# A selective scan with a routed feed-forward: u and the softplus sums transposed apart, and their product made in place out of PSUM

## The chip, the cores and the metric

One core of a Trainium2 chip runs the whole block. The metric is device time in microseconds. A core has five engines that run their own instruction streams in order and meet at semaphores: TensorE (PE, matrix products and transposes, results in PSUM), VectorE (DVE), ScalarE (ACT, activations), GpSimd (POOL) and SyncE (SP, which issues DMAs here).

## The reference, cut to what matters

```python
def step(state, inp):                      # over time, for each of 4 batches
    d, b, c, u = inp                       # d = softplus(dt), u = silu(conv(x))
    dA = jnp.exp(d[..., None] * A)         # 512 channels x 16 states
    state = state * dA + (d * u)[..., None] * b[:, None, :]
    y = jnp.einsum('bdn,bn->bd', state, c)
    return (state, y)
...
y = (moveaxis(ys) + D[None, :, None] * x) * silu(z)
x = x + tanh(g_xattn[0]) * y               # then x + tanh(g_ffn[0]) * (16 experts, 2 of them per token, + shared)
```

`d` comes from a rank 16 projection: `dt = softplus(dt_proj_w @ dt_low + dt_proj_b)`. All of it is fp32, 4 batches of 512 time steps.

## The kernel before, in words

The first half of the kernel is the scan. Channels stand on the 128 partitions in four groups j, time along the free dimension (512). A batch has 64 items i = 4n + j, for state n (16) and group j (4), and each engine has its part of an item:

- ScalarE makes `dA` of the item from `dts` (L1162, `decay`), and after the decay of j = 2 the inputs of the whole state n: `dbuT = duT * B`, four operations with time on the partitions (L1173, `input_terms`). That is why d*u is needed transposed, as `duT`.
- TensorE transposes `dbuT` back to channels, into one of two PSUM banks `dbu_ps` (L767, `step`), then adds the product of the item five before (LAG = 5) to `y_ps` by a transpose (L785, `add_y`), then does what `pieces` has for the item.
- VectorE scans, `hst = scan(dA, dbu_ps)` (L1476), then its `pieces`.
- GpSimd multiplies by C, `prod = hst * cbc` (L573, `products`). `prod` has four slots, so the product of item i waits until TensorE has added that of item i-4. `dA` and `hst` have eight, so ScalarE can be eight items ahead of VectorE.

While batch b is scanned, the `pieces` of items 8 to 63 prepare batch b+1 in two PSUM banks of their own, `mp[0]` and `mp[1]`: convolution and projection (items 8 to 34), silu (ScalarE, item 40), the projection to dt, B and C (`x_proj`, 37 to 40), and then for each group j the softplus and d*u. Each bank is used in a fixed order: a use begins when the one before is read (`bank_free`, `misc_full`, `misc_read`; `HEAD`, `LOOP`, `ut_use`, `bt_use`, `dut_use` number the uses). For group j, with the items at which each engine has its part in the kernel before:

- `dt_proj` (TensorE, L742, items 42, 46, 50, 54) into `mp[0]`.
- `softplus_parts` (ScalarE, L1135 to L1141, items 46, 50, 54, 58): abs, relu, exp, log. It waits for the sum dt of two groups before.
- `round_part` (VectorE, L1452, items 44, 48, 52, 56) makes `sp_t`, and `log_part` (GpSimd, L554 and L557, after the product of the same items) corrects the logarithm by it.
- `dt_part` (VectorE, L1458, items 48, 52, 56, 60): `dts = sp_r + sp_l`.
- `du_part` (VectorE, L1469, items 49, 53, 57, 61): `du = dts * xs`, where `xs` is u.
- `du_transposes` (TensorE, L749, items 50, 54, 58, 62) into `mp[1]`, and `du_to_time` (ScalarE, L1145, items 57, 61 and items 0 and 1 of the next batch) copies them to `duT`.

`b_transposes` (TensorE, item 42) and `b_to_sbuf` (VectorE, item 43) bring B to `BT` through `mp[1]`. `skip_part` (GpSimd, after the batch) multiplies `xs` by D in place. At items 2 to 5 of the next batch VectorE finishes the batch before (`post`, L1485). Batches 0 to 2 are one loop on each engine (`Fori`), batch 3 is written out after it and has no preparation. The second half of the kernel, the experts, comes after all of this.

Of the kernel before, what the change touches and what calls it, by code (L numbers as in the profile page):

```python
# [18 lines left out]
def flamingo_block(nc, x, ctx_in, g_xattn, g_ffn, in_proj_w, conv_w, conv_b, x_proj_w, dt_proj_w,  # L19
# [33 lines left out]
    with ExitStack() as top:  # L53
# [31 lines left out]
        xs = s1("xs", [P, ND, L])  # L85
        sp_t = s1("sp_t", [P, L])
        sp_u = s1("sp_u", [P, 2, L])
# [238 lines left out]
        HEAD0, HEAD1 = 8, 8  # L326
        LOOP0, LOOP1 = 7, 13

# [12 lines left out]
        def dt_use(bp):  # L341

            return bp * LOOP0 + HEAD0 - 4

        def bt_use(bp):
# [187 lines left out]
        def _(pool):  # L533
# [16 lines left out]
            def log_part(bp, j):  # L550

                q = bp * ND + j
                pool.wait_ge(sp_round, q + 1)
                pool.tensor_tensor(sp_t[:], sp_t[:], sp_u[:, j % 2, :], ALU.subtract).then_inc(sp_err, 1)  # L554
                pool.wait_ge(sp_ln, q + 1)
                pool.wait_ge(sp_err, q + 1)
                pool.tensor_tensor(sp_l[:, j % 2, :], sp_l[:, j % 2, :], sp_t[:],  # L557
                                   ALU.subtract).then_inc(sp_log, 1)

            def skip_part(bp):  # L560
                pool.wait_ge(du_ready, (bp + 1) * ND)
                pool.sem_inc(wait_carrier, 1)
                for j in range(ND):
                    pool.tensor_scalar(xs[:, j, :], xs[:, j, :], Dv[:, j:j + 1], 1.0, ALU.mult,
                                       ALU.mult).then_inc(skip_ready, 1)

            def products(b, n, bp=None):
                pool.wait_ge(c_loaded[n % 2], 16 * (b * (NS // 2) + n // 2 + 1))
                for j in range(ND):
                    i = b * ITEMS + n * ND + j  # L570
                    pool.wait_ge(scanned, i + 1 + RING)
                    pool.wait_ge(prod_used, i + 1)
                    pool.tensor_tensor(prod[:, prod_slot(n, j), :], hst[:, slot_of(n, j), :], cbc[:, n % 2, :],  # L573
                                       ALU.mult).then_inc(prod_ready, 1)
                    if bp is not None and 11 <= n < 15 and j == 0:
                        log_part(bp, n - 11)

# [101 lines left out]
        def _(pe):  # L679
# [64 lines left out]

            def du_transposes(use, bp, j):
                pe.wait_ge(du_ready, bp * ND + j + 1)
                bank_free(1, use)
                for t in range(NL):
                    last = tr(mp[1][:, t * P:(t + 1) * P], du[:, j % 2, t * P:(t + 1) * P], ident[:])  # L749
                last.then_inc(misc_full[1], 1)  # L750
# [38 lines left out]
            def pieces(b, n, j):  # L789
# [19 lines left out]
                if 37 <= i < 41:  # L809
                    x_proj(xp_use(bp), bp, i - 37, i - 36)  # L810
                if 10 <= n < 14 and j == 2:
                    dt_proj(dt_use(bp) + n - 10, n - 10)
                if i == 42:
                    b_transposes(bt_use(bp), bp)
                if 12 <= n < 16 and j == 2:
                    du_transposes(dut_use(bp) + n - 12, bp, n - 12)

# [54 lines left out]
            first_steps(0)  # L872
            with pe.Fori(0, NB - 1) as b:
                for n in range(2, NS):
# [198 lines left out]
        def _(act):  # L1073
# [68 lines left out]

            def du_to_time(bp, j):
                act.wait_ge(misc_full[1], dut_use(bp) + j + 1)
                nc.scalar.copy(par(duT, bp)[:, :, j * P:(j + 1) * P],  # L1145
# [42 lines left out]
            def pieces(bp, n, j):  # L1188
# [5 lines left out]
                if i == 40:  # L1194
                    silus(bp, (misc_read[0], base0(b) + 3))
                if 11 <= n < 15 and j == 2:
                    softplus_parts(bp, n - 11)
                if 14 <= n < 16 and j == 1:
                    du_to_time(bp, n - 14)
                if n == 0 and j < 2:  # L1200
                    du_to_time(bp, j + 2)

# [35 lines left out]
            with act.Fori(0, NB - 1) as b:  # L1238
                for n in range(2, NS):
                    step(b, n, b + 1)  # L1240
                step(b + 1, 0, b + 1)
                step(b + 1, 1)
# [124 lines left out]
        def _(dve):  # L1367
# [78 lines left out]
            def round_part(bp, j):  # L1446

                q = bp * ND + j
                if not (isinstance(q, int) and q < 1):
                    dve.wait_ge(sp_log, q)  # L1450
                dve.wait_ge(sp_exp, q + 1)
                V.tensor_scalar(sp_t[:], sp_u[:, j % 2, :], 1.0, -1.0, ALU.add, ALU.add).then_inc(sp_round, 1)  # L1452

# [6 lines left out]

            def du_part(bp, j):

                q = bp * ND + j
                dve.wait_ge(dt_ready, q + 1)
                dve.wait_ge(silu_done, bp + 1)
                if j >= 2:
                    dve.wait_ge(misc_full[1], dut_use(bp) + j - 1)
                dve.sem_inc(wait_carrier, 1)
                V.tensor_tensor(du[:, j % 2, :], par(dts, bp)[:, j, :], xs[:, j, :], ALU.mult).then_inc(du_ready, 1)  # L1469

# [24 lines left out]
            def pieces(b, n, j):  # L1495
# [16 lines left out]
                if i == 41:  # L1512
                    x_proj_to_sbuf(bp)
                if i == 43:
                    b_to_sbuf(bp)
                if 11 <= n < 15 and j == 0:
                    round_part(bp, n - 11)
                if 12 <= n < 16 and j == 0:
                    dt_part(bp, n - 12)
                if 12 <= n < 16 and j == 1:  # L1520
                    du_part(bp, n - 12)

# [398 lines left out]
```

## Time and profile before

| | us |
|---|---|
| median of 3 runs | 1107.25 (1105.29 to 1111.7) |
| the profiled execution | 1106.53 |
| its span | 1104.9 |
| first scan / last scan of the first half begins | 60.0 / 512.3 |
| busy: PE / DVE / ACT / POOL | 920.2 / 728.1 / 611.2 / 594.0 |

The span is what the profile covers. Busy time is summed over the whole span, and the two halves of the kernel have different limits: the scan half ends at about 521 us. In timelines a row starts with its start and its duration, neighbouring operations of one kind are merged (x4), and what stands in brackets is the idle time before and what ended it.

### The profile page before, as it was taken

What the parts mean: (1) busy time and instruction counts of PE and PEld (TensorE: products, weight loads), DVE (VectorE), ACT (ScalarE), POOL (GpSimd) and SP (SyncE); (2) the same over time, 40 slices, a digit from 0 to 9 for tenths busy, and PEclk for the clock granted to TensorE, in tenths of its full rate; (3) what the DMA queues carried; (4) which work ended last, traced back from release to release, by engine and by line L of the source; (5) the groups of instructions that cost most, each with busy time, mean ns of one, the idle gap of its engine ahead of it and who ended that gap; (6) DMA issues with size and microseconds to landing.
All of it is one profiled execution on the core that took longest, in us unless ns stands there. A gap on an engine that the chain in (4) does not pass through costs nothing.

```text
span 1104.9 us, 22746 instructions
## 1 busy us (share of the span) xinstructions
PE 920.2 (83%) x5388; PEld 776.6 (70%) x5389; DVE 728.1 (66%) x1023; ACT 611.2 (55%) x1037; POOL 594.0 (54%) x521
## 2 busy tenths in 40 slices
PE   6589876998689877974799989699999999973787
PEld 3267655765567566753799979698988898862775
DVE  4769798878888788998544467354544545444467
ACT  4697997599778977993322222243444544432211
POOL 4557796878967796996100007334344424420254
PEclk9579998999999978998899999899999999995789
DMA  8105111331105113110311118645556656653376
GB/s 254 40 20 191 59 36 33 138 109 30 39 28 199 49 29 109 56 48 20 117 38 38 51 36 296 242 137 204 184 197 216 216 203 233 206 176 111 116 220 236
DMA packets 67432, 137.08 MB, mean 124 GB/s; under 512 B 9392, under 2 KB 15024, under 8 KB 67248
## 3 DMA queue, kind: packets, MB, share of 16 engines
q1 hardware_dynamic: 54736, 105.66, 28.5%
q0 software_dynamic: 8960, 29.37, 7.4%
q10 hardware_dynamic: 3680, 1.39, 0.6%
q8 instruction: 24, 0.39, 0.1%
q14 instruction: 32, 0.26, 0.1%
HBM read 163.53 MB, written 42.07 MB: 186 GB/s over the span
## 4 chain that ended last, share of the span: by engine, by line
PE 40%; issue 4%; DVE 4%; POOL 3%; DMA 1%; ACT 1%; DVEq 0%; POOLq 0%
PE psY L956 12%; PE psG L920 11%; PE psU L920 10%; PE psT L913 3%; POOL slot_in L625 3%; PE psHT L934 3%; DVE x_tok L1864 1%; ACT xh L1290 1%; DMA gbuf<-slot_out,posi 0%; PE dbu_ps L767 0%; DVE hl L1676 0%; DVEq L1841 0%; DVE xl L1682 0%; PE y_ps L785 0%; POOL gbuf L672 0%
## 5 line engine op out<-in xcount | busy, mean ns | idle before, releaser
L573 POOL TENSOR_TENSOR prod<-hst,cbc 128x512 f32<-128x512 f32 x256 | 333.0, 1327 | 84.8 <-PE y_ps L785 66.9
L1476 DVE TENSOR_TENSOR_SCAN hst<-dA,dbu_ps 128x512 f32<-128x512 f32 x256 | 304.0, 1208 | 67.8 <-PE dbu_ps L767 57.8
L767 PE MATMUL dbu_ps<-ident,dbuT 128*128 128x128 f32 x1024 | 169.9, 292 | 38.5 <-ACT dbuT L1173 16.8
L767 PEld LDWEIGHTS dbu_ps<-ident,dbuT 128*128 128x128 f32 x1024 | 124.9, 149 | 104.6 <-issue 49.7
L1296 ACT CAST hh<-psHT 128x384 fp32r<-128x384 f32 x79 | 37.8, 478 | 288.8 <-PE psHT L934 288.8
L1162 ACT ACTIVATE dA<-dts,Aneg 128x512 f32 (+1 forms) x256 | 169.3, 712 | 33.2 <-DVE hst L1476 32.7
L1173 ACT ACTIVATE dbuT<-duT,BT 128x512 f32 (+1 forms) x256 | 163.0, 709 | 0.0
L785 PE MATMUL y_ps<-ident,prod 128*128 128x128 f32 x1024 | 160.7, 284 | 2.1 <-POOL prod L573 2.0
L920 PE MATMUL psG<-weights,xh 128*128 (+1 forms) x560 | 142.3, 337 | 14.8 <-issue 8.5
L956 PE MATMUL psY<-weights,hh 128*128 (+3 forms) x420 | 135.7, 405 | 16.7 <-DVE hl L1676 14.3
L920 PE MATMUL psU<-weights,xh 128*128 (+2 forms) x560 | 143.1, 337 | 0.0
L785 PEld LDWEIGHTS y_ps<-ident,prod 128*128 128x128 f32 x1024 | 127.6, 148 | 3.3 <-POOL prod L573 3.3
L920 PEld LDWEIGHTS psG<-weights,xh 128*128 128x128 f32 x560 | 104.2, 197 | 25.1 <-issue 16.5
L660 POOL DMA_DIRECT2D slot_out<-yout x48 | 26.3, 547 | 171.6 <-DVE yout L1697 171.6
L1676 DVE TENSOR_TENSOR hl<-psHT,hh 128x384 fp32r<-128x384 f32 x80 | 44.4, 555 | 99.9 <-ACT hh L1296 99.4
L956 PEld LDWEIGHTS psY<-weights,hh 128*128 128x128 f32 (+1 forms) x420 | 77.1, 190 | 35.1 <-issue 12.9
L920 PEld LDWEIGHTS psU<-weights,xh 128*128 128x128 f32 x560 | 96.1, 191 | 0.0
L920 PE MATMUL psG<-weights,xl 128*128 (+1 forms) x280 | 93.5, 334 | 0.0
L920 PE MATMUL psU<-weights,xl 128*128 (+2 forms) x280 | 91.2, 326 | 0.0
L1246 ACT CAST weights<-raw_gu 128x704 f32 (+1 forms) x76 | 53.9, 778 | 55.7 <-PE psY L956 30.5
L956 PE MATMUL psY<-weights,hl 128*128 (+3 forms) x210 | 83.1, 396 | 0.0
L1697 DVE COPY yout<-psY 128x512 f32<-128x512 f32 x48 | 33.2, 692 | 73.8 <-PE psY L956 65.8
(220 smaller groups left out, 1389.4 us busy)
## 6 DMA issues: line engine op xcount, KB each, us to landing
raw_gu<-in_L_ffn_w_gate_up_dram SPq DMA_DIRECT2D x100, 704.0 KB
raw_d<-in_L_ffn_w_down_dram SPq DMA_DIRECT2D x50, 512.0 KB
cbc<-c_rows SPq DMA_DIRECT2D x64, 256.0 KB, 3.2
slot_in<-ztile SPq DMA_DIRECT2D x3, 4096.0 KB, 13.7
gbuf<-slot_in SPq DMA_DIRECT2D x48, 256.0 KB, 3.1
slot_out<-yout POOLq DMA_DIRECT2D x48, 256.0 KB, 3.2
raw_d<-in_L_ffn_w_down_dram SPq DMA_DIRECT2D x50, 192.0 KB
xn_rows<-xin SPq DMA_DIRECT2D x16, 256.0 KB, 2.0
```

The source lines that it names most:

```text
L573: pool.tensor_tensor(prod[:, prod_slot(n, j), :], hst[:, slot_of(n, j), :], cbc[:, n % 2, :], ALU.mult).then_inc(prod_ready, 1)
L767: last = tr(dbu_ps[j % 2][:, t * P:(t + 1) * P], dbuT[:, n % 2, t, j * P:(j + 1) * P], ident[:])
L785: last = mm(y_ps[t][:, j * P:(j + 1) * P], prod[:, prod_slot(n, j), t * P:(t + 1) * P], ident[:], start=False, stop=m == ITEMS - 1, is_tra ...
L920: last = mm(ps[:, 0:width], a[:, k, c, :], w_at(w, buf)[:, c, w0:w0 + width], start=n == 0, stop=n == 3 * KH - 1)
L956: last = mm(psY[k][:], a[0:rows, k, c, :], w_at(w, buf)[0:rows, c, :], start=n == 0, stop=n == 8)
L1162: nc.scalar.activation(dA[:, slot_of(n, j), :], par(dts, b)[:, j, :], ACT.Exp, scale=Aneg[:, j, n:n + 1]).then_inc(da_ready, 1)
L1173: last = nc.scalar.activation(dbuT[:, n % 2, t, :], par(duT, b)[:, t, :], ACT.Copy, scale=par(BT, b)[:, t, RK + n:RK + n + 1])
L1246: nc.scalar.copy(dst(wgu_h)[:, c, 0:2 * INTER], raw_gu[:, c, :]).then_inc(gu_hi, 1)
L1296: nc.scalar.copy(hh[:, 1 - k, :, :], psHT[:, 0:3, :]).then_inc(hh_ready, 1)
L1476: V.tensor_tensor_scan(hst[:, slot_of(n, j), :], dA[:, slot_of(n, j), :], dbu_ps[j % 2][:], 0.0, ALU.mult, ALU.add).then_inc(scanned, 1)
L1676: V.tensor_tensor(hl[:, k, :, :], psHT[:, 0:3, :], hh[:, k, :, :].bitcast(F32), ALU.subtract).then_inc(hl_ready, 1)
L1697: ins = V.tensor_copy(yout[:, k, :], psY[k][:])
```

## The change

- TensorE transposes u (`xs`) and, later, the sums dt (`dts`), not the product du: `u_transposes` at items 41, 43, 44 and 46, `dt_transposes` at 51, 54, 57 and 60, all through `mp[1]`, which so has 17 uses in a batch and not 13.
- ScalarE copies u's transposes to `duT` (`u_to_time`, items 45, 47, 48, 51).
- VectorE multiplies in place: `duT = mp[1] * duT` (`dut_part`, items 52, 55, 58, 61). `du_part` goes; the buffer `du` now holds what `sp_t` held, in two parts.
- The blocks of the four groups stand three items apart, not four: `dt_proj` 42, 45, 48, 51; softplus 46, 49, 52, 55; rounding and logarithm 44, 47, 50, 53; `dt_part` 48, 51, 54, 57. `b_transposes` goes to 49, `b_to_sbuf` to 50.
- `skip_part` waits for the transposes of u.
- TensorE's loop over batches 0 to 2 is written out.

```diff
-        LOOP0, LOOP1 = 7, 13
+        LOOP0, LOOP1 = 7, 17
+        def ut_use(bp):
+            return bp * LOOP1 + HEAD1 - 9
...
-                pool.tensor_tensor(sp_t[:], sp_t[:], sp_u[:, j % 2, :], ALU.subtract).then_inc(sp_err, 1)
+                pool.tensor_tensor(du[:, j % 2, :], du[:, j % 2, :], sp_u[:, j % 2, :], ALU.subtract).then_inc(sp_err, 1)
...
-                pool.wait_ge(du_ready, (bp + 1) * ND)
+                if isinstance(bp, int):
+                    pool.wait_ge(du_ready, ND)
+                else:
+                    pool.wait_ge(misc_full[1], ut_use(bp) + ND)
...
-                    if bp is not None and 11 <= n < 15 and j == 0:
-                        log_part(bp, n - 11)
+                    if bp is not None and n * ND + j in (44, 47, 50, 53):
+                        log_part(bp, (n * ND + j - 44) // 3)
...
-            def du_transposes(use, bp, j):
-                pe.wait_ge(du_ready, bp * ND + j + 1)
+            def u_transposes(use, bp, j):
                 bank_free(1, use)
+                pe.wait_ge(silu_done, bp + 1)
+                pe.sem_inc(wait_carrier, 1)
                 for t in range(NL):
-                    last = tr(mp[1][:, t * P:(t + 1) * P], du[:, j % 2, t * P:(t + 1) * P], ident[:])
+                    last = tr(mp[1][:, t * P:(t + 1) * P], xs[:, j, t * P:(t + 1) * P], ident[:])
+                last.then_inc(misc_full[1], 1)
+
+            def dt_transposes(use, bp, j):
+                pe.wait_ge(dt_ready, bp * ND + j + 1)
+                bank_free(1, use)
+                pe.sem_inc(wait_carrier, 1)
+                for t in range(NL):
+                    last = tr(mp[1][:, t * P:(t + 1) * P], dts[:, bp % 2, j, t * P:(t + 1) * P], ident[:])
                 last.then_inc(misc_full[1], 1)
...
-                if 10 <= n < 14 and j == 2:
-                    dt_proj(dt_use(bp) + n - 10, n - 10)
-                if i == 42:
+                if i in (42, 45, 48, 51):
+                    jj = (i - 42) // 3
+                    dt_proj(dt_use(bp) + jj, jj)
+                if i in (41, 43, 44, 46):
+                    jj = (41, 43, 44, 46).index(i)
+                    u_transposes(ut_use(bp) + jj, bp, jj)
+                if i == 49:
                     b_transposes(bt_use(bp), bp)
-                if 12 <= n < 16 and j == 2:
-                    du_transposes(dut_use(bp) + n - 12, bp, n - 12)
+                if i in (51, 54, 57, 60):
+                    jj = (i - 51) // 3
+                    dt_transposes(dut_use(bp) + jj, bp, jj)
...
-            with pe.Fori(0, NB - 1) as b:
+            for b in range(NB - 1):
...
-            def du_to_time(bp, j):
-                act.wait_ge(misc_full[1], dut_use(bp) + j + 1)
+            def u_to_time(bp, j):
+                act.wait_ge(misc_full[1], ut_use(bp) + j + 1)
...
-                if 11 <= n < 15 and j == 2:
-                    softplus_parts(bp, n - 11)
-                if 14 <= n < 16 and j == 1:
-                    du_to_time(bp, n - 14)
-                if n == 0 and j < 2:
-                    du_to_time(bp, j + 2)
+                if i in (46, 49, 52, 55):
+                    softplus_parts(bp, (i - 46) // 3)
+                if i in (45, 47, 48, 51):
+                    u_to_time(bp, (45, 47, 48, 51).index(i))
...
-            def du_part(bp, j):
-
-                q = bp * ND + j
-                dve.wait_ge(dt_ready, q + 1)
-                dve.wait_ge(silu_done, bp + 1)
-                if j >= 2:
-                    dve.wait_ge(misc_full[1], dut_use(bp) + j - 1)
+            def dut_part(bp, j):
+
+                dve.wait_ge(misc_full[1], dut_use(bp) + j + 1)
                 dve.sem_inc(wait_carrier, 1)
-                V.tensor_tensor(du[:, j % 2, :], par(dts, bp)[:, j, :], xs[:, j, :], ALU.mult).then_inc(du_ready, 1)
+                block = par(duT, bp)[:, :, j * P:(j + 1) * P]
+                V.tensor_tensor(block, mp[1][:].rearrange("p (t d) -> p t d", t=NL), block,
+                                ALU.mult).then_inc(misc_read[1], 1)
...
-                if i == 43:
+                if i == 50:
                     b_to_sbuf(bp)
-                if 11 <= n < 15 and j == 0:
-                    round_part(bp, n - 11)
-                if 12 <= n < 16 and j == 0:
-                    dt_part(bp, n - 12)
-                if 12 <= n < 16 and j == 1:
-                    du_part(bp, n - 12)
+                if i in (44, 47, 50, 53):
+                    round_part(bp, (i - 44) // 3)
+                if i in (48, 51, 54, 57):
+                    dt_part(bp, (i - 48) // 3)
+                if i in (52, 55, 58, 61):
+                    dut_part(bp, (i - 52) // 3)
```

## Rows read from the trace of the kernel before

**Rows 1.** The page: busy time of each engine, share of the span.
```profile
PE 920.2 (83%) x5388; PEld 776.6 (70%) x5389; DVE 728.1 (66%) x1023; ACT 611.2 (55%) x1037; POOL 594.0 (54%) x521
```
**Rows 2.** Busy by stretch: length; PE, PEld, DVE, ACT, POOL; clock; DMA share; GB/s.
```profile
136.14:176.86 40.72, 26.74 (x180) 21.25 (x181) 35.67 (x34) 34.57 (x59) 39.58 (x29) 0.96 0.11 34
257.81:298.52 40.71, 27.59 (x180) 22.59 (x181) 35.03 (x33) 34.67 (x59) 39.58 (x29) 0.92 0.10 33
378.11:418.96 40.85, 29.92 (x180) 25.14 (x181) 34.01 (x34) 34.67 (x59) 39.71 (x29) 0.83 0.12 32
```
**Rows 3.** Waits from 257.81 to 298.52 us: total, times, longest.
```profile
PE mp L749 <- DVE du L1469: 8.9, 4, 2.9
ACT duT L1145 <- PE mp L749: 5.9, 2, 4.8
...
POOL prod L573 <- PE y_ps L785: 1.5, 1, 1.5
```
**Rows 4.** Groups of instructions, same stretch: busy, mean ns | idle before.
```profile
L554 POOL TENSOR_TENSOR sp_t<-sp_t,sp_u 128x512 f32<-128x512 f32 x4 | 6.5, 1634 | 0.0
L1458 DVE TENSOR_TENSOR dts<-sp_r,sp_l 128x512 f32 x4 | 6.1, 1525 | 0.0
L557 POOL TENSOR_TENSOR sp_l<-sp_l,sp_t 128x512 f32<-128x512 f32 x4 | 5.1, 1272 | 0.6
L1452 DVE TENSOR_SCALAR sp_t<-sp_u 128x512 f32<-128x512 f32 x4 | 4.0, 996 | 0.0
...
L1469 DVE TENSOR_TENSOR du<-dts,xs 128x512 f32<-128x512 f32 x4 | 2.6, 660 | 0.0
```
**Rows 5.** Groups of instructions of the first 620 us, VectorE's product from PSUM.
```profile
L1485 DVE TENSOR_TENSOR y_ps<-y_ps,zT 128x512 f32<-128x512 f32 x16 | 9.9, 688 | 2.4 <-PE y_ps L785 2.4
```
**Rows 6.** Timeline of ScalarE: start, duration, operation [idle before].
```profile
249.53 2.55 ACT L1162 ACTIVATE dA<-dts,Aneg 128x512 f32 x4
251.99 2.54 ACT L1173 ACTIVATE dbuT<-duT,BT 128x512 f32 x4
255.66 0.69 ACT L1135 ACTIVATE sp_u<-mp,db 128x512 f32<-128x512 f32 x1 [1.14 <-PE mp L742]
...
258.02 2.55 ACT L1162 ACTIVATE dA<-dts,Aneg 128x512 f32 x4
260.48 2.54 ACT L1173 ACTIVATE dbuT<-duT,BT 128x512 f32 x4
```
**Rows 7.** Timeline of TensorE, transposes of items 42 and 44.
```profile
252.70 0.60 PE L767 MATMUL dbu_ps<-ident,dbuT 128*128 128x128 f32 x4
...
256.67 0.60 PE L767 MATMUL dbu_ps<-ident,dbuT 128*128 128x128 f32 x4
```
**Rows 8.** Timeline of VectorE, scans 44, 45 to 47, and 48.
```profile
257.81 1.21 DVE L1476 TENSOR_TENSOR_SCAN hst<-dA,dbu_ps 128x512 f32<-128x512 f32 x1
...
259.69 3.43 DVE L1476 TENSOR_TENSOR_SCAN hst<-dA,dbu_ps 128x512 f32<-128x512 f32 x3
263.84 1.22 DVE L1476 TENSOR_TENSOR_SCAN hst<-dA,dbu_ps 128x512 f32<-128x512 f32 x1 [0.73 <-PE dbu_ps L767]
```
**Rows 9.** Timelines of ScalarE, TensorE and VectorE across the batch's end.
```profile
294.05 0.59 ACT L1145 COPY duT<-mp 128x512 f32 x1 [4.84 <-PE mp L749]
...
295.16 2.54 ACT L1173 ACTIVATE dbuT<-duT,BT 128x512 f32 x4
...
297.83 0.65 PE L767 MATMUL dbu_ps<-ident,dbuT 128*128 128x128 f32 x4 [3.03 <-ACT dbuT L1173]
...
298.52 2.33 DVE L1476 TENSOR_TENSOR_SCAN hst<-dA,dbu_ps 128x512 f32<-128x512 f32 x2 [2.90 <-PE dbu_ps L767]
```
**Rows 10.** Busy by stretch, one inside batch 1's tail.
```profile
269.10:272.40 3.30, 2.58 (x12) 2.59 (x13) 2.30 (x4) 3.27 (x6) 3.16 (x4) 0.50 0.20 56
```
**Rows 11.** DMA queues from 60 to 180 us: packets, MB, share of 16 engines.
```profile
q8 instruction: 6, 0.10, 0.3%
```
**Rows 12.** The same from 180 to 440 us, where q8 has no row.
```profile
q14 instruction: 8, 0.07, 0.1%
```

More of the change, by code:

```diff
@@ L85, in flamingo_block @@
         xs = s1("xs", [P, ND, L])
-        sp_t = s1("sp_t", [P, L])
         sp_u = s1("sp_u", [P, 2, L])
@@ L553, in log_part @@
                 pool.wait_ge(sp_round, q + 1)
-                pool.tensor_tensor(sp_t[:], sp_t[:], sp_u[:, j % 2, :], ALU.subtract).then_inc(sp_err, 1)
+                pool.tensor_tensor(du[:, j % 2, :], du[:, j % 2, :], sp_u[:, j % 2, :], ALU.subtract).then_inc(sp_err, 1)
                 pool.wait_ge(sp_ln, q + 1)
                 pool.wait_ge(sp_err, q + 1)
-                pool.tensor_tensor(sp_l[:, j % 2, :], sp_l[:, j % 2, :], sp_t[:],
+                pool.tensor_tensor(sp_l[:, j % 2, :], sp_l[:, j % 2, :], du[:, j % 2, :],
                                    ALU.subtract).then_inc(sp_log, 1)
             def skip_part(bp):
-                pool.wait_ge(du_ready, (bp + 1) * ND)
+                if isinstance(bp, int):
+                    pool.wait_ge(du_ready, ND)
+                else:
+                    pool.wait_ge(misc_full[1], ut_use(bp) + ND)
                 pool.sem_inc(wait_carrier, 1)
@@ L1240, in _ @@
                     step(b, n, b + 1)
-                step(b + 1, 0, b + 1)
+                step(b + 1, 0)
                 step(b + 1, 1)
@@ L1448, in round_part @@
                 q = bp * ND + j
-                if not (isinstance(q, int) and q < 1):
-                    dve.wait_ge(sp_log, q)
+                dve.wait_ge(sp_log, q - 1)
                 dve.wait_ge(sp_exp, q + 1)
-                V.tensor_scalar(sp_t[:], sp_u[:, j % 2, :], 1.0, -1.0, ALU.add, ALU.add).then_inc(sp_round, 1)
+                V.tensor_scalar(du[:, j % 2, :], sp_u[:, j % 2, :], 1.0, -1.0, ALU.add, ALU.add).then_inc(sp_round, 1)
             def dt_part(bp, j):
```

## The prediction

> **What bounds the kernel now.** Items are numbered i = 4n + j inside a batch: state n, channel group j, one scan each. The page first [rows 1]: no engine is full over the span, not even TensorE with 83%, and the two halves of the kernel have different limits. So the question is which engine is full where the change acts. The change touches items 41 to 63 of batches 0 to 2, and the first two items of the next batch; the last batch and the expert part keep their work. I call the stretch from scan 44 to the first scan of the next batch the tail. The busy table by stretch [rows 2] gives its length three times: 40.72, 40.71 and 40.85 us. GpSimd is busy 39.6 of it, VectorE and ScalarE about 35, TensorE 27 to 30. The granted clock was 0.96, 0.92 and 0.83 in the three, and their length hardly moved: TensorE doesn't set it.
>
> The waits of that tail [rows 3] show what the old order costs TensorE: 8.9 us for the four du products, and ScalarE 5.9 us for their transposes. They look like the gain. But what is queued behind them is GpSimd, which hardly rests, so taking them away gives at most what GpSimd can give back.
>
> Then I read the durations of the tail [rows 4]. The same 128x512 operation on GpSimd takes 1272 ns at line 557 and 1634 ns at line 554; VectorE's two-input operation takes 660 ns at line 1469 and 1525 ns at line 1458. Both engines wait for one another: a VectorE operation that finds a GpSimd one under way ends after it. The Trainium skill ("SBUF — State Buffer", Who interferes with whom) says the same of VectorE operations with two SBUF inputs or in a two-port mode, that the later one fully blocks, and that one with a single SBUF input doesn't contend; the trace agrees. By that rule the new product, read from PSUM, is free of this wait, while rounding and sum keep it.
>
> **The change part by part.** Three batches, so each figure per batch counts three times. The product moves: four multiplications of 660 ns leave [rows 4], four from PSUM come, nearest row 688 ns [rows 5], so VectorE's own work stays. GpSimd sheds what du cost it at line 554, 4 x (1634 - 1272) = 1.4 us. ScalarE's four copies move from items 57 to 65 to items 45 to 51. TensorE gets 16 more transposes, 4 x 0.45 us (four last 0.60 with the end that overlaps the next, [rows 7]), beside idle time of its own. The sums t in du's buffer instead of sp_t: nothing. No DMA is moved, and SyncE's waits count uses that come before the new ones. The preparation of batch 0 stays.
>
> What must be worked out is the new order, since every engine runs in order. I follow batch 1 by the clock of the trace.
>
> 1. ScalarE [rows 6]. It runs four items ahead and reached the end of decay 45 at about 251.4 (the third of the four from 249.53). There the new copy of u(0) waits for TensorE's u(0) transposes. TensorE's item 41 ends where item 42 starts now, 252.70 [rows 7]; transposes and their end: 253.3. The copy takes 0.5 (0.59 and overlapped, [rows 9]), decay 0.6, dbuT of state 11 2.45: it ends at 257.0 instead of 254.5, and softplus(0) starts there instead of at 255.66.
> 2. TensorE's step 44 waits for that dbuT, 257.17 instead of 256.67 [rows 7]. Behind it stands u(2), which needs the bank of u(1), and ScalarE copies u(1) only after softplus(0) (2.35 us from 255.66 to 258.02, [rows 6]) and decay 47: bank free at 260.5. Queued behind it on TensorE are step 45 and the y of item 40, for which GpSimd's product 44 waits. So step 45 comes at 261.1, scan 45 at 261.75 and not at 259.69 [rows 8], product 44 at 262.2.
> 3. Softplus(1) now stands ahead of dbuT of state 12 on ScalarE; today it stands behind. It waits for dt_proj(1), behind step 45: 263.1. Then 2.35 + decay 0.6 + dbuT 2.45: 268.5. Today that dbuT ran 260.48 to 263.0 [rows 6]. Step 48 starts at 268.75, scan 48 at 269.45; today 263.84 [rows 8]. That is 5.6 us late, and TensorE stood idle from about 265.0.
> 4. GpSimd: product 47 needs the y of item 43, behind step 48: 269.95 to 271.2. dt sum (0) at item 48 waits for it and ends at 271.65, and softplus(2) waits for that sum: 271.75 to 274.1. Two decays and dbuT of state 13: 277.75. Scan 52 at 278.55, some 5.4 us late.
> 5. From there nothing waits for du. VectorE has scans 52 to 61, ten at 1.14 (the three from 259.69 took 3.43 in all, [rows 8]), four products at 0.58 (660 ns less some 0.08 by which neighbours overlap), rounding (3) at 0.65 (996 ns is a mean with waits in it; I take it for an operation like the product), sums (2) and (3) at 0.58: 11.4 + 2.3 + 0.65 + 1.15 = 15.5, to 294.05 without a collision. Then dbuT(0) of the next batch, 2.45 with 0.1 on each side, and TensorE's transposes 0.65 [rows 9]: scan 64 at 297.35. Today it starts at 298.52 [rows 9]. So without a collision the tail gains 1.2.
> 6. Collisions: rounding (3) and sums (2) and (3) meet a GpSimd that works without a break (10 products and 8 softplus operations now within 10 items). Each can wait up to one operation, 1.24 (1272 ns less the overlap): 3.7 together at most, to 301.05. Laying GpSimd's operations out from 271.65 at 1.24 each, rounding (3) waits 0.7, the sums 1.1 and 0.9: scan 64 at some 300.0, which is 1.5 late. The ends are -1.2 and +2.5; this layout hangs on phases of a few tenths, so I take +1.0, between it and the middle (+0.65).
>
> The head of the next batch (dbuT of state 1 behind that of state 0) shifts as a whole, and nothing in it is slower. The longer TensorE stream: batch 0 fetched six blocks of instructions of 16 KB in the 120 us to 180 [rows 11], and after that up to 440 us the queue isn't among those that moved anything: the instruction packets of that time are another queue's [rows 12]. Yet the tails of batches 0 and 1 took 40.72 and 40.71 us. I cost writing it out at nothing; exposed, a block would be 0.3% x 16 x 120 / 6 = 1.0 us.
>
> Sum: the profiled execution took 1106.53 us (span 1104.9), 0.7 below the median of the three, 1107.25. 1106.5 + 3 x 1.0 = 1109.5; on the median's scale 1110.
>
> **Rivals.**
> A, the forecast: as above, -3.6 to +7.5 for three batches, 1103.6 to 1114.7 us. For it: ScalarE goes from 255.66 to 263.0 without a break already today [rows 6], so three copies and a softplus put ahead of dbuT must delay it. Chance 0.55.
> B, slower: the idle TensorE before step 48 (3.7 us) is followed by a stretch at the lower clock, and the collisions come as laid out. The trace has such a place: 269.1 to 272.4 ran at 0.50, that is 1.2 GHz [rows 10], about the end of the first wait for du. Today that costs nothing, since GpSimd is the bound [rows 2]. After the change step 48, its y and dt_proj(2) stand on the path: product 47 and so sum (0) come 0.8 later. +2.3 a batch, 1114 us. It decides above +1.85 a batch. Against: not each idle stretch was followed by a low clock. Chance 0.25.
> C, faster: ScalarE is in fact far enough ahead that u and softplus hide, and GpSimd alone is left. It then saves 1.4 us of waits for du and its 1.5 us of idleness at the end [rows 3]: -3.0 a batch, 1098 us. Against it stands step 2, where the bank of u(1) is free only after softplus(0). Chance 0.15.
> D, the instruction blocks aren't hidden: twelve more for batches 1 and 2, each 1.0 us: +11.5 on the forecast, 1121 us. Against it are the equal tails. Chance 0.05.
> That the change doesn't do what it says is within A: the products do leave du, but the waits come back elsewhere.
>
> **How the numbers follow.** 0.5% of 1107.25 is 5.5 us, about what a measurement of this kernel tells from no change. Faster by more is C: 0.15. Slower by more is B, D and the top of A (0.04): 0.34. Within: 0.51. The likeliest is A: 1110 us. The range 1098 to 1116 takes in C's value and B's, and leaves D out, half of C below it and a part of B above.
>
> **What would show it.** In the profile after: the wait of TensorE for du is gone, and in its place TensorE waits some 2.5 us for ScalarE's copy of u(1) at item 44 and some 3.7 us for dbuT at item 48, in each batch (step 2, 3). ScalarE waits 1.9 us for the first u transposes. Scan 48 follows scan 44 by 11.7 us (6.0 today). From scan 48 to scan 64 it takes 28 to 31.6 us (34.7 today, [rows 8, 9]). GpSimd's product 44 waits for y. The waits at rounding and sum tell of the collisions (step 6). If scan 48 isn't late, steps 1 to 3 are wrong and C stands; if the tail is the same but batches 1 and 2 differ from batch 0 in their first 40 items, it is D. The prediction would be wrong on the other side if each dt sum were to wait for its logarithm as well.

## The result, and the profile after

| | before | changed |
|---|---|---|
| median of 15 runs, us | 1106.7 | 1113.74 |
| lowest to highest | 1102.34 to 1111.7 | 1109.58 to 1116.35 |
| ratio, fast runs to fast runs | | 1.0063, 95% interval 1.0047 to 1.008 |
| span of the profiled execution | 1104.9 | 1110.7 |

The kernel became slower by 7 us, 0.6%. The two profiled executions differ by 5.8 us. Of these 1.3 us lie after batch 3's last scan (592.6 us before, 593.9 after, from the start of scan 63 of batch 3 to the end of the span); the other 4.5 us are in the scan half. By the starts of the scans, in us:

| | before: batch 0, 1, 2 | changed: batch 0, 1, 2 |
|---|---|---|
| scan 44 to 48 | 6.0, 6.0, 6.0 | 13.5, 12.9, 13.0 |
| scan 48 to 52 | 8.3, 9.3, 9.7 | 11.3, 10.0, 10.0 |
| scan 52 to 64 | 26.4, 25.4, 25.1 | 20.3, 20.3, 20.2 |
| tail (44 to 64) | 40.7, 40.7, 40.9 | 45.0, 43.2, 43.2 |
| head of the next batch (64 to 72) | 18.2, 16.9, 18.5 | 16.9, 16.9, 17.1 |

The tails lost 9.1 us in all. The heads gave back 2.6, batch 0's first eight items 0.8, and batch 3's scans 8 to 63 1.5 (74.9 to 73.4). Items 8 to 44 take 62.7 to 62.8 us in both.

The page's busy row of the changed kernel, against [rows 1]:

```profile
PE 930.0 (84%) x5436; PEld 779.2 (70%) x5437; DVE 722.0 (65%) x1023; ACT 611.6 (55%) x1037; POOL 588.1 (53%) x521
```

The three tails by stretch, in the columns of [rows 2], and two parts of batch 1's:

```profile
135.50:180.54 45.04, 32.78 (x196) 25.71 (x195) 34.13 (x33) 35.71 (x60) 36.57 (x29) 0.85 0.11 31
260.26:303.44 43.18, 32.98 (x196) 25.89 (x195) 33.77 (x33) 35.73 (x60) 36.45 (x29) 0.84 0.10 32
383.15:426.32 43.17, 32.97 (x196) 25.89 (x195) 33.72 (x33) 35.72 (x60) 36.41 (x29) 0.84 0.10 31
264.30:270.90 6.60, 6.60 (x25) 4.72 (x23) 2.78 (x3) 4.65 (x9) 5.03 (x4) 0.50 0.04 11
283.18:303.44 20.26, 13.76 (x110) 11.63 (x109) 18.68 (x19) 17.20 (x29) 19.97 (x16) 1.00 0.14 40
```

GpSimd sheds 3.1 us in a tail (39.58 to 36.45), more than the 1.4 that were worked out, and the tail is 2.5 longer. So GpSimd's work didn't set this tail. Its four operations on `du` fell only from 6.5 to 6.0 us, its 21 products from 29.1 to 27.4.

ScalarE's timeline through the same tail shows where it now stands idle (start, duration, operation, idle before and what ended it):

```profile
255.86 0.59 ACT L1165 COPY duT<-mp 128x512 f32 x1 [1.93 <-PE mp L756]
...
259.42 0.67 ACT L1155 ACTIVATE sp_u<-mp,db 128x512 f32<-128x512 f32 x1
...
266.95 0.69 ACT L1155 ACTIVATE sp_u<-mp,db 128x512 f32<-128x512 f32 x1 [1.92 <-PE mp L748]
...
275.78 0.69 ACT L1155 ACTIVATE sp_u<-mp,db 128x512 f32<-128x512 f32 x1 [1.62 <-DVE dts L1475]
...
300.13 2.56 ACT L1193 ACTIVATE dbuT<-duT,BT 128x512 f32 x4 [3.02 <-PE dbu_ps L782]
```

The copy of u(0), ahead of scan 44, waits 1.93 us for its transposes, softplus(1) 1.92 for dt_proj(1), softplus(2) 1.62 for the sum of group 0, and the first dbuT of the next batch 3.02, until VectorE's last product (299.16 to 299.82 in the rows of VectorE below; the profile names another releaser). ScalarE's waits as a list (total, times, longest), for the tail of batch 1:

```profile
ACT dbuT L1193 <- PE dbu_ps L782: 3.0, 1, 3.0
ACT sp_u L1155 <- DVE dts L1475: 2.1, 2, 1.6
ACT sp_u L1155 <- PE mp L748: 1.9, 1, 1.9
ACT duT L1165 <- PE mp L756: 0.3, 1, 0.3
```

That is 7.3 us; 35.73 busy and 7.3 waiting make 43.0 of the 43.18. Before, ScalarE was busy for 34.67 [rows 2] and waited 5.9 [rows 3], 40.6 of 40.71. Such a sum doesn't name the engine that sets a tail, since an engine is either busy or idle. TensorE's closes as well: before, it was busy for 27.59 us, waited 8.9 for du [rows 3] and in two more rows 4.2, 40.7 in all.

```profile
PE dbu_ps L767 <- ACT dbuT L1173: 3.0, 1, 3.0
PE dbu_ps L767 <- DVE hst L1476: 1.2, 2, 0.9
```

What sets a tail has to come from the experiments. Nor did ScalarE get more work. Its 35.73 us of batch 1 are 1.06 more than before because the stretch is cut at scan 44, and most of softplus(0) now lies behind that cut (259.42 to 261.8) and lay ahead of it before (255.66 to 258.1, with scan 44 at 257.81). The copies are fewer in it, 3 for 4 (before, then changed):

```profile
L1145 ACT COPY duT<-mp 128x512 f32 x4 | 2.3, 575 | 5.9 <-PE mp L749 5.9
L1165 ACT COPY duT<-mp 128x512 f32 x3 | 1.7, 570 | 0.3 <-PE mp L756 0.3
```

In the whole span ScalarE has 1037 operations in both kernels, 611.2 us before [rows 1] and 611.6 here.

TensorE's timeline where it goes wrong, with dt_proj(0), the transposes of u(2), step 45, and dt_proj(1):

```profile
256.70 1.12 PE L748 MATMUL mp<-xdbl,dpT 16*128 16x512 f32 x2
...
263.07 0.63 PE L756 MATMUL mp<-ident,xs 128*128 128x128 f32 x4 [2.41 <-ACT duT L1165]
263.54 0.60 PE L782 MATMUL dbu_ps<-ident,dbuT 128*128 128x128 f32 x4
...
264.72 2.07 PE L748 MATMUL mp<-xdbl,dpT 16*128 16x512 f32 x2
```

And VectorE's timeline, scans 45 and 46, the sum of group 3, the last product, and scan 64:

```profile
264.17 1.22 DVE L1491 TENSOR_TENSOR_SCAN hst<-dA,dbu_ps 128x512 f32<-128x512 f32 x1 [1.81 <-PE dbu_ps L782]
267.88 1.22 DVE L1491 TENSOR_TENSOR_SCAN hst<-dA,dbu_ps 128x512 f32<-128x512 f32 x1 [2.48 <-PE dbu_ps L782]
...
292.75 1.43 DVE L1475 TENSOR_TENSOR dts<-sp_r,sp_l 128x512 f32 x1
...
299.16 0.66 DVE L1483 TENSOR_TENSOR duT<-mp,duT 128x512 f32 x1
...
303.44 1.22 DVE L1491 TENSOR_TENSOR_SCAN hst<-dA,dbu_ps 128x512 f32<-128x512 f32 x1 [1.39 <-PE dbu_ps L782]
```

The u(2) transposes stand 2.41 us on the bank of u(1), and step 45 behind them. Then the granted clock is 0.50 (1.2 GHz) from 264.3 on, the last stretch but one above, and dt_proj(1) takes 2.07 us where dt_proj(0), at the higher clock (2.4 GHz), took 1.12.

### The profile page after: what moved, and what is told of

It is laid out like the page before. It is cut to its first block, busy times and chain, and to the rows that moved or that the text cites. A ratio compares the mean times of both kernels' runs of the same rounds, so it can differ in the third digit from the quotient of the medians.

```text
span 1110.7 us, 22589 instructions
## 1 busy us (share of the span) xinstructions
PE 930.0 (84%) x5436; PEld 779.2 (70%) x5437; DVE 722.0 (65%) x1023; ACT 611.6 (55%) x1037; POOL 588.1 (53%) x521
## 4 chain that ended last, share of the span: by engine, by line
PE 55%; ACT 12%; issue 12%; DVE 8%; POOL 5%; ACTq 1%; DMA 1%; DVEq 1%; SPq 0%; POOLq 0%
PE psY L976 12%; PE psG L940 11%; PE psU L940 10%; PE dbu_ps L782 5%; PE y_ps L800 4%; ACT dbuT L1193 4%; ACT dA L1182 4%; PE psT L933 3%; PE mp L724 3%; DVE hst L1491 3%; POOL slot_in L631 3%; PE psHT L954 2%; POOL prod L579 2%; PE y_ps L791 1%; PE mp L734 1%
## 5 line engine op out<-in xcount | busy, mean ns | idle before, releaser
L579 POOL TENSOR_TENSOR prod<-hst,cbc 128x512 f32<-128x512 f32 x256 | 327.8, 1307 | 95.6 <-PE y_ps L800 79.1
L940 PEld LDWEIGHTS psG<-weights,xh 128*128 128x128 f32 x560 | 105.0, 199 | 24.9 <-issue 16.4
L1691 DVE TENSOR_TENSOR hl<-psHT,hh 128x384 fp32r<-128x384 f32 x80 | 44.5, 556 | 101.0 <-ACT hh L1314 100.6
L1712 DVE COPY yout<-psY 128x512 f32<-128x512 f32 x48 | 33.2, 692 | 75.2 <-PE psY L976 66.0
## 6 DMA issues: line engine op xcount, KB each, us to landing
slot_in<-ztile SPq DMA_DIRECT2D x3, 4096.0 KB, 13.5
```

Of the source, the lines that this page charges most:

```text
L940: last = mm(ps[:, 0:width], a[:, k, c, :], w_at(w, buf)[:, c, w0:w0 + width], start=n == 0, stop=n == 3 * KH - 1)
L1691: V.tensor_tensor(hl[:, k, :, :], psHT[:, 0:3, :], hh[:, k, :, :].bitcast(F32), ALU.subtract).then_inc(hl_ready, 1)
```

## The experiments

Each is an edit of the kernel before or of the changed one; ratios are to the kernel before, run on the same chip. Tails and waits are those of batch 1 unless said. The chips differed (the kernel before took 1132.5, 1129.1 and 1105.2 us in the three series), so only ratios and the lengths of tails, which agree on all chips, are compared.

### TensorE's loop written out, alone

```diff
-            with pe.Fori(0, NB - 1) as b:
+            for b in range(NB - 1):
```

> The kernel before with TensorE's loop over batches 0 to 2 written out and nothing else. If the slowdown comes from the order of the pieces (my theory), this is the time of before: ratio 0.999 to 1.001, the three tails 40.7 us each, and some ten 16 KB instruction blocks more on the queue q8. If instruction blocks aren't hidden (rival), batches 1 and 2 grow by up to 6 us each, ratio up to 1.010, and TensorE idles with nothing to wait for.

Ratio 0.9994 (0.9974 to 1.0015), tails 40.8, 40.6, 40.6. The page's row of the queue of instruction blocks has 33 packets for 24:

```profile
q8 instruction: 33, 0.54, 0.2%
```

So rival D falls. The nine further blocks (twelve were worked out) are hidden, and the step that costed them at nothing was right.

### Is it GpSimd? The correction of the logarithm left out, before and after

```diff
                 q = bp * ND + j
-                pool.wait_ge(sp_round, q + 1)
-                pool.tensor_tensor(sp_t[:], sp_t[:], sp_u[:, j % 2, :], ALU.subtract).then_inc(sp_err, 1)
                 pool.wait_ge(sp_ln, q + 1)
-                pool.wait_ge(sp_err, q + 1)
-                pool.tensor_tensor(sp_l[:, j % 2, :], sp_l[:, j % 2, :], sp_t[:],
-                                   ALU.subtract).then_inc(sp_log, 1)
+                pool.sem_inc(sp_log, 1)
```

> The kernel before with GpSimd's two operations of the logarithm's correction left out in batches 1 to 3 (the sum takes the uncorrected logarithm): 8 operations of 1.24 us a batch less on GpSimd, everything else in its place. If GpSimd sets the tail before the change, it falls from 40.7 to 33 to 38 us. If it is TensorE's wait for du, it stays above 39.5.

> The changed kernel with GpSimd's two operations of the logarithm's correction left out in batches 1 to 3 (the sum takes the uncorrected logarithm). Theory of collisions: with 8 operations fewer, rounding and sums seldom meet a GpSimd at work, and the stretch from scan 52 to scan 64 falls from 20.3 us to 18 to 19. Theory that these waits are covered by others: it stays at 20 us or more. The stretch from scan 44 to 52 (22.9 us) is ScalarE's and TensorE's and stays within 1 us in either.

Both kernels compute a less exact logarithm in batches 1 to 3 and were executed once, so they have tails and no ratio. The tail of the kernel before, with 11 us less work on GpSimd, in the columns of [rows 2]:

```profile
258.63:300.36 41.73, 27.88 (x180) 22.87 (x181) 35.78 (x34) 34.67 (x59) 28.22 (x21) 0.92 0.10 32
```

And the one row of ScalarE's waits in it, with VectorE's sums (the form of [rows 4]):

```profile
ACT duT L1141 <- PE mp L745: 7.0, 2, 5.4
...
L1454 DVE TENSOR_TENSOR dts<-sp_r,sp_l 128x512 f32 x4 | 6.6, 1654 | 0.0
```

GpSimd is busy for 28.2 of 41.7 us, and the tail is 1.0 longer, not shorter (41.8 and 41.8 in the other two). ScalarE has the same 34.67 and waits longer for the transposes of du. This is the run against the first reading of the prediction: the amount of GpSimd's work alone doesn't hold the tail. It doesn't clear GpSimd of everything, because the collisions are still there. VectorE's sums take 1654 ns in the mean, and took 1525 [rows 4]; they now meet GpSimd's products.

In the changed kernel it is the same: tails 44.5, 43.5 and 44.7 us, 0.5 shorter, 0.3 longer and 1.5 longer, scan 52 to 64 in batch 1 20.5 us where 18 to 19 was expected. The four sums, changed and then without the correction:

```profile
L1475 DVE TENSOR_TENSOR dts<-sp_r,sp_l 128x512 f32 x4 | 4.2, 1046 | 0.0
L1471 DVE TENSOR_TENSOR dts<-sp_r,sp_l 128x512 f32 x4 | 4.3, 1066 | 0.0
```

So this run didn't take the collisions away either, and can't tell what they cost.

### The two parts of the change apart

Blocks three items apart, with du made and transposed as before. The edit of ScalarE's softplus is shown; the other engines' items, edited in the same way, stand in the expectation, and so do the copies of du, which move to items 57, 60, 62 and 0:

```diff
-                if 11 <= n < 15 and j == 2:
-                    softplus_parts(bp, n - 11)
+                if i in (46, 49, 52, 55):
+                    softplus_parts(bp, (i - 46) // 3)
```

> The kernel before with one part of the change alone: blocks three items apart (dt_proj 42, 45, 48, 51; softplus 46, 49, 52, 55; rounding 44, 47, 50, 53; sums 48, 51, 54, 57; du one item behind its sum, its transposes at 50, 53, 56, 59, their copies at 57, 60, 62 and item 0 of the next batch), du made by VectorE and transposed as before. Softplus(1) so stands ahead of dbuT of state 12. Theory that this place is what costs: scan 48 follows scan 44 by 8 to 9.5 us (6.0 before), and the tail is 41 to 43 us, ratio 1.001 to 1.006. Theory that the u transposes cost: the tail is at or below 40.7, ratio 0.998 to 1.000.

Ratio 1.0033 (1.0003 to 1.0062). The tail by stretch:

```profile
256.06:299.22 43.16, 31.97 (x182) 26.73 (x182) 35.68 (x33) 35.63 (x60) 38.38 (x29) 0.80 0.10 31
```

ScalarE's waits in it:

```profile
ACT duT L1145 <- PE mp L749: 3.2, 1, 3.2
ACT sp_u L1135 <- PE mp L742: 3.0, 1, 3.0
ACT sp_u L1135 <- DVE dts L1458: 1.2, 1, 1.2
```

In batch 1 the nearer spacing alone gives the tail of the whole change, 43.2 us, without one transpose of u. The waits are of the kinds of the change, one group later: softplus(2) waits 3.0 us for dt_proj(2), and softplus(3) 1.2 for the sum of group 1. In batches 0 and 2 the tails are 42.1 and 42.5 (45.0 and 43.2 in the change), so of the 9.1 us that the three tails lost it makes 5.4. The ratio lies half way; its heads were 16.4, 16.7 and 17.6 us (18.2, 16.9 and 18.5 before). Scan 48 came 9.0 us after scan 44, as expected.

Then the other part, the product in place with blocks four items apart:

```diff
-                if i in (42, 45, 48, 51):
-                    jj = (i - 42) // 3
+                if i in (42, 46, 50, 54):
+                    jj = (i - 42) // 4
                     dt_proj(dt_use(bp) + jj, jj)
-                if i in (41, 43, 44, 46):
-                    jj = (41, 43, 44, 46).index(i)
+                if i in (44, 47, 53, 57):
+                    jj = (44, 47, 53, 57).index(i)
...
-                if i in (51, 54, 57, 60):
-                    jj = (i - 51) // 3
+                if i in (50, 54, 58, 62):
+                    jj = (i - 50) // 4
```

> The product in place out of PSUM as in the change, but the blocks of the four groups four items apart as before (softplus 46, 50, 54, 58; rounding 44, 48, 52, 56; sums 48, 52, 56, 60; B's transposes back at 42), and the u transposes spread between them (TensorE 44, 47, 53, 57; copies on ScalarE 48, 51, 57, 62; products at 51, 55, 59, 62). If the loss comes from softplus and copies put ahead of dbuT, nothing of it is left here and GpSimd sheds what du cost it: tail 38 to 40 us (40.7 before, 43.2 after), ratio 0.992 to 0.998. If transposing u and dt apart costs by itself (16 more transposes, a bank of 17 uses), the tail is 41 to 43 us and the ratio 1.001 to 1.006.

Ratio 1.0033 (1.001 to 1.0056), tail 41.8, in batches 0 and 2 40.4 and 41.8: a miss for the order's numbers, and within those of its rival, that transposing u and dt apart costs by itself. Its trace named a place that can tell the two apart. TensorE's timeline before the transposes of the third sum:

```profile
287.24 1.09 PE L766 MATMUL mp<-ident,dts 128*128 128x128 f32 x4 [4.24 <-ACT duT L1167]
```

ScalarE's waits in that tail, all of them ahead of the next batch's first dbuT:

```profile
ACT dbuT L1195 <- DVE duT L1485: 6.8, 1, 6.8
```

The copy of u(3) stood behind the dbuT of state 15 on ScalarE and held the bank. One item sooner, with u(3) transposed at 56 and the last product at 61:

```diff
-                if i in (44, 47, 53, 57):
+                if i in (44, 47, 53, 56):
...
-                if i in (48, 51, 57, 62):
+                if i in (48, 51, 57, 61):
...
-                if i in (51, 55, 59, 62):
+                if i in (51, 55, 59, 61):
```

> The product in place with blocks four items apart, as in the run before it, but without the two waits that its trace showed: ScalarE copies u(3) at item 61, ahead of dbuT of state 15 (TensorE transposes it at 56 and had waited 4.2 us for that copy), and VectorE multiplies the last group at item 61 in place of 62. Theory of order: both waits go, tail 37.5 to 39.5 us (41.8 there, 40.7 before), ratio to before 0.993 to 0.997. Theory that the way by PSUM costs by itself: the tail stays above 40.7, ratio 1.000 or more.

Ratio 0.9944 (0.9922 to 0.9967), tails 38.3, 37.7 and 37.7. Batch 1's by stretch:

```profile
254.87:292.55 37.68, 29.14 (x196) 22.71 (x197) 34.87 (x34) 34.48 (x59) 36.91 (x29) 0.95 0.13 36
```

And ScalarE's waits in it:

```profile
ACT dbuT L1195 <- PE dbu_ps L784: 3.1, 1, 3.1
```

ScalarE waits once, and the rival, that the way by PSUM costs by itself, falls. This kernel beats the kernel before and, by the two ratios, the changed one by 1.2%. With the blocks four items apart and u(3) copied ahead of the dbuT of state 15, the three tails are 2.4, 3.0 and 3.2 us shorter than before. What sets the tail now is open: GpSimd is busy for 36.9 of the 37.7 us, 2.7 less than before, and ScalarE for 34.5. The correction of the logarithm was not left out of this kernel, which would tell.

### Which of the new places costs

Softplus(1) behind the dbuT of state 12:

```diff
-                if i in (46, 49, 52, 55):
-                    softplus_parts(bp, (i - 46) // 3)
+                if i in (46, 50, 52, 55):
+                    softplus_parts(bp, (46, 50, 52, 55).index(i))
```

> The changed kernel with one edit: softplus(1) at ScalarE's item 50 in place of 49, so behind dbuT of state 12; all u transposes and copies as in the change. If the place of softplus(1) closes the loop dbuT(12) - step 48 - sum(0) - softplus(2) - dbuT(13), then dbuT(13) ends some 3.5 us earlier, the tail is 39.6 to 40.8 us (43.2 in the change) and the ratio 0.998 to 1.000; scan 48 then waits for rounding (1), which waits for the exponential. If the bank of u(1) at item 44 is the cause, the tail stays above 42 and the ratio above 1.003.

Ratio 1.0018 (0.9996 to 1.0041), tail 42.5, in batches 0 and 2 42.6 and 42.4. Neither expectation: less came back than the loop promised (39.6 to 40.8 us).

u(2) behind step 45:

```diff
-                if i in (41, 43, 44, 46):
-                    jj = (41, 43, 44, 46).index(i)
+                if i in (41, 43, 45, 46):
+                    jj = (41, 43, 45, 46).index(i)
```

> The changed kernel with one edit: TensorE transposes u(2) at item 45 in place of 44, so behind step 45, the y of item 40 and dt_proj(1). The wait for the bank then holds none of them. Theory of order, with both causes adding: softplus(1) starts 2.1 us earlier, scan 48 follows scan 44 by 10.8 us (12.9), the tail is 41 us, ratio 1.000 to 1.003. If softplus(1)'s place alone counts, the tail stays at 43 us and the ratio at 1.005 or more.

Ratio 1.0052 (1.0032 to 1.0072), tail 43.7, in batches 0 and 2 42.9 and 43.2. Scan 48 came after 11.4 us (10.8 expected, 12.9 in the change), and the tails of batches 1 and 2 didn't shorten: the 1.6 us came back as a wait further on. Both edits together:

> Both single edits together: u(2) behind step 45, softplus(1) behind dbuT of state 12. If the two causes add, the tail is 38 to 39.5 us, ratio 0.993 to 0.997. If they are one chain, it is that of the better of the two alone, within 0.5 us.

Ratio 0.9992 (0.9969 to 1.0014), tail 41.2, in batches 0 and 2 40.6 and 40.4. That is neither the 38 to 39.5 us of two causes that add nor the better of the two alone within 0.5. The three tails are 122.2 us, 122.3 in the kernel before and 131.4 in the change: these two places account for the whole loss of the tails. ScalarE's waits in the tail with softplus(1) behind (waits of 0.3 left out here and below):

```profile
ACT dbuT L1193 <- PE dbu_ps L782: 3.4, 1, 3.4
ACT sp_u L1155 <- DVE dts L1475: 2.7, 1, 2.7
```

With u(2) later:

```profile
ACT dbuT L1193 <- PE dbu_ps L782: 3.9, 1, 3.9
ACT sp_u L1155 <- PE mp L748: 2.5, 1, 2.5
ACT sp_u L1155 <- DVE dts L1475: 1.0, 1, 1.0
```

With both:

```profile
ACT dbuT L1193 <- PE dbu_ps L782: 3.9, 1, 3.9
ACT sp_u L1155 <- DVE dts L1475: 0.9, 1, 0.9
```

With one edit each softplus(2) still waits, for the sum of group 0 or for dt_proj(2); with both, that wait shrinks to 0.9. So softplus(1) behind gives 0.7 and 0.8 in batches 1 and 2, u(2) later -0.5 and 0.0, both together 2.0 and 2.8 (in batch 0, whose tail was 45.0, they give 2.4, 2.1 and 4.4). The loop of the prediction's steps 3 and 4 (dbuT(12), step 48, sum (0), softplus(2), dbuT(13)) is there, but it isn't the only path.

An edit that moved more of u shows the same (u(2) at 47 and u(3) at 48, copy of u(2) at 50):

```diff
-                if i in (41, 43, 44, 46):
+                if i in (41, 43, 47, 48):
...
-                if i in (45, 47, 48, 51):
+                if i in (45, 47, 50, 51):
```

> The changed kernel with the transposes of u(2) and u(3) at TensorE's items 47 and 48 in place of 44 and 46, and the copy of u(2) at ScalarE's item 50 in place of 48. Theory of order: the 3 us that TensorE waits at item 44 for the bank of u(1) are gone, scan 45 follows scan 44 by under 2 us (3.9 now), scan 48 follows scan 44 by 9 to 11 us (12.9 now), and 1.5 to 2.5 us a batch of the change's loss come back: ratio 0.9995 to 1.002. Theory of collisions (the loss is made by rounding and sums that meet a GpSimd without a break after item 52): the tail stays at 43 us, ratio 1.006.

> The same with softplus(1) at ScalarE's item 50 too, so behind dbuT of state 12 (copy of u(2) behind it, before it no change). Theory of order: scan 48 comes another 2 us earlier, 7 to 9 us after scan 44, but ScalarE's work up to dbuT of state 13 is the same, so scan 52 and the tail stay as in the run with u(2) later, within 0.7 us a batch: ratio within 0.002 of it. If what counts is the place of softplus(1) alone, another 2 us a batch come back: ratio 0.994 to 0.997.

The first had a ratio of 1.0062 (1.0039 to 1.0086) and a tail of 43.2, with scan 48 after 10.5 us: the copy of u(3) now waited 4.1 us for its transposes behind step 48. These are the numbers of the rival expectation, that the collisions make the loss, and this run alone doesn't refute it. The second, with softplus(1) behind as well, had 0.9991 (0.9968 to 1.0015) and tails of 39.5, 40.6 and 40.4: one softplus moved on one engine, and nothing of the work near the end. I had expected the two to be equal, because ScalarE's work is the same; its waits weren't.

### The clock

```diff
+                    if i == 44:
+                        pe.wait_ge(scanned, b * ITEMS + 44 + RING)
+                        for r in range(5):
+                            for t in range(NL):
+                                tr(dbu_ps[1][:, t * P:(t + 1) * P], dbuT[:, 1, t, P:2 * P], ident[:])
```

> The changed kernel, with the transposes of item 45 made five times over (20 transposes, 2.2 us) by TensorE at item 44, ahead of its wait for the bank of u(1); they write what step 45 writes again. Theory of the clock: TensorE then has no idle stretch at item 44, the granted clock stays at 1.0 through items 45 to 48, scan 48 follows scan 44 by 11.5 us and not 12.9, and 1 to 1.5 us a batch come back: ratio 1.001 to 1.004. If the lower clock there costs nothing, the tail stays at 43.2 and the ratio at 1.006.

Ratio 1.0057 (1.0033 to 1.0081), tails 42.3, 43.8 and 44.1. TensorE's timeline:

```profile
258.31 2.35 PE L835 MATMUL dbu_ps<-ident,dbuT 128*128 128x128 f32 x20
260.89 0.63 PE L756 MATMUL mp<-ident,xs 128*128 128x128 f32 x4 [0.23 <-ACT duT L1170]
...
262.32 1.12 PE L748 MATMUL mp<-xdbl,dpT 16*128 16x512 f32 x2
...
269.16 1.11 PE L782 MATMUL dbu_ps<-ident,dbuT 128*128 128x128 f32 x4 [3.39 <-ACT dbuT L1198]
```

The idle stretch at item 44 is filled, dt_proj(1) takes 1.12 us and not 2.07, and scans 46 and 47 come sooner (7.3 us after scan 44 for scan 47, 10.2 in the change). But TensorE then waits 3.39 us at step 48, and from there the transposes take 1.11 where they took 0.66 (the granted clock is 0.50 from 268.4 on for 10 us). The stretch at the lower clock moved from one wait to the next one, and the tails didn't follow: batch 0's is 2.8 us shorter, the other two 0.6 and 0.9 longer. What the lower clock costs with ScalarE's order as it is, alone, no run here shows.

## Why the prediction was right or wrong

The range (1098 to 1116) held the time, and the direction of the forecast was right; the size wasn't. The forecast was 2.75 us over the median of before, within what can be told from no change, and the measured step is 7.0, slower beyond it. The case that came true is nearest to rival B, which had 0.25. That its 1114 is the measured time to within 0.3 us is luck: the tails lost 9.1 us (3 x 2.3 = 6.9 in B), and 4.9 came back in places that no case counted.

- What bounds the kernel: wrong as it stands. The prediction took GpSimd, busy for 39.6 of 40.7 us [rows 2], for the bound of the tail. Without eight of its operations the tail was no shorter; ScalarE then waited 7.0 us for the transposes of du, which fits the other expectation of that run, that the way of du holds the tail. With the product moved and the blocks four items apart the tail fell by 3.0 us and GpSimd's busy time by 2.7, which fits the limit that the prediction named. So GpSimd's work alone is not the bound; that it and the way of du hold the tail together is a reading, and not shown. The sum of the prediction goes along the order of the pieces, and not by this bound, except where GpSimd's products delay the sum in step 4 and in step 6.
- That the granted clock didn't matter before (0.96, 0.92, 0.83 and equal tails) was right as a fact; the reason given for it falls with GpSimd. What takes its place, that TensorE's waits for du leave room, was only argued.
- Step 1: right. ScalarE waited 1.93 us for the first u transposes (1.9 worked out).
- Step 2: right. TensorE waited 2.41 for the bank of u(1) (2.5), and scan 45 came 3.91 us after scan 44 (3.94). Product 44 waited for y, 2.9 us.
- Step 3: the order was right, the size short. Softplus(1) waited 1.92 us for dt_proj(1), some 0.9 by the prediction's own times (decay 49 ends at 262.2, dt_proj(1) at 263.1), since TensorE ran at 1.2 GHz at that point: 2.07 for 1.12 us. Scan 48 came after 12.9 us (11.65). Rival B had this mechanism after step 48, worth 0.8; it struck at item 45. At step 48 TensorE waited 1.3 us and not 3.7, because the lower clock had kept it busy until 271.2; only in the run that filled the first wait was it 3.39.
- Step 4: right in kind, softplus(2) waited for the sum of group 0: 1.62 us. The sum itself ended at 275.6, 2.4 after scan 48 began (2.2 worked out). Scan 52 came 10.0 us after scan 48 (9.1): step 52 stood behind dt_proj(3), which took 1.36 us with part of it at the lower clock, and the transposes of the first sum.
- Step 5: right. From scan 52 to scan 64 20.26 us were measured, between 18.8 without a collision and 22.5.
- Step 6: the collisions are there and smaller than laid out (2.7). The sum of group 3 took 1.43 us for 0.66, rounding (3) 0.85 where it took 0.50 in the run without the correction, and the sum of group 2 met none: 1.1 us. With some 0.2 in which scan 56 waited for TensorE, and 0.3 more from the last product to scan 64, that makes 20.4, near the 20.3 measured. Whether less of them would shorten the tail no run shows.
- The copies: the prediction costed moving ScalarE's four copies at nothing, and that held. All four ran ahead of scan 64 before the change too (the last at 294.05, [rows 9]).
- Sum per batch, by batch 1: +1.0 was forecast, half a us below its own layout (+1.5). Steps 3 and 4 came 1.3 and 0.9 longer than worked out, steps 5 and 6 1.2 shorter: 2.5. In batch 2 it was 2.3 and in batch 0 4.3, 9.1 in all, less 4.9 elsewhere. In batch 0 the lower clock lay for 10.2 us from 148.2 on, after a first stretch at 137.9; whether that is why its tail is the longest, no run tells. The heads' gain of 1.3 and 1.4 us goes with the clock: the mean granted clock in the heads after batches 0, 1 and 2 was 0.72, 0.90 and 0.72 before, and 0.90 in all three of the change, and the middle one is as long as before. The 1.5 us in batch 3 stay open; its scans 8 to 63 took 73.3 us in the run with the blocks three apart alone and 75.0 and 75.1 in those with four, but also 75.2 in the changed kernel without the correction, so the spacing alone doesn't explain them.
- Rival C fell in the form given (softplus(1) and (2) and the bank of u(1) were not hidden), and yet its number, 3.0 a batch, is what the product in place gives with blocks four apart: 2.4, 3.0 and 3.2. GpSimd shed 2.7 us there in batch 1. Rival D fell by the first run.

## What to carry to other kernels

The engine that is busiest in a stretch need not be the one that sets it. Take as the bound only what changes the length when it is moved or left out; here the fullest row (97%) could lose more than a quarter of its work for nothing. Busy time plus waits makes up the stretch for every engine, so this sum checks the reading of a trace and finds no bound. When pieces are placed by hand into streams that run in order, ask first what each one is put ahead of. The blocks three items apart, with a softplus ahead of the operand that everyone waits for, cost 5.4 us in three tails; the kernel with sixteen more transposes a batch and the old spacing had tails 8.6 us shorter. Two waits in one loop are tested together, since each alone may come back as the other.

## What the runs showed of the hardware that I had not expected

Filling an idle stretch of TensorE didn't keep its clock: the stretch at 1.2 GHz followed the next wait instead (3.39 us, then the transposes took 1.11 us for 0.66). In the changed kernel an idle stretch of 2.41 us was followed by one at 1.2 GHz of some 6.8 us, though it began 1.1 us after work had started again.

Eight GpSimd operations fewer in a tail of the kernel before didn't shorten VectorE's collisions. Its two-input sum took 1525 ns in the mean with them and 1654 without, since GpSimd's products remained to be met; the shortest in these tails took 660.
